# Scan kernel: softplus sums, one-hots, B and a product move to other places and engines

## What is computed

```python
h = layernorm(x);  u, z = split(in_proj(h))           # 256 channels each
uc = silu(causal_conv4(u) + conv_b)
dt, Bm, Cm = split(x_proj(uc))                         # 64, 16, 16
delta = softplus(dt_proj(dt) + dt_bias)
deltaA   = exp(delta * A)                              # 256 channels x 16 states
deltaB_u = delta * Bm * uc
state_t  = deltaA_t * state_{t-1} + deltaB_u_t;  y_t = sum_n state_t * Cm_t
out = out_proj((y + uc * D) * silu(z)) + x
# then: layernorm, 8 experts (128 -> 512 -> 128, gelu), the best two of each token, layernorm
```

## Time and profile before

| | |
|---|---|
| median of 3 runs | 890.92 us (889.49 to 892.53) |
| the profiled execution | 889.88 us, its span 888.0 us |
| VectorE busy | 696.1 us, 78% of the span |
| TensorE busy | 671.0 us, 76% |
| GpSimd busy | 541.4 us, 61% |
| ScalarE busy | 423.7 us, 48% |
| scans (line 1296) | 256, 315.2 us, 1268 ns each |
| inflow (line 1286) | 63, 142.9 us, 2268 ns each |
| times_c (line 533) | 128, 305.9 us, 2395 ns each |
| decay (line 1062) | 256, 164.3 us, 660 ns each |

### The profile page before, as it was taken

The page is one execution under the profiler, slowest core; times in us unless marked ns, Lnnn a source line. Parts: engine busy times, 40 slices in busy tenths (PEclk is TensorE's granted clock), DMA queues, the critical chain, the costliest instruction groups (busy, mean ns, idle before and its releaser), DMA issues. The chain is left out here.

```text
span 888.0 us, 12242 instructions
## 1 busy us (share of the span) xinstructions
PE 671.0 (76%) x2905; PEld 307.3 (35%) x2905; DVE 696.1 (78%) x1350; ACT 423.7 (48%) x884; POOL 541.4 (61%) x526
## 2 busy tenths in 40 slices
PE   3777968797789869878887977887732999999920
PEld 2322212232222223223222222222221888888820
DVE  2167699998998898899889899999732677677754
ACT  3527558366455635736554563334210554445425
POOL 5107547665786776778777677777863455455433
PEclk8876888867886786787787665557555899999975
DMA  3085276374476846627645555565003566566645
GB/s 82 0 203 130 48 163 145 80 178 111 94 176 153 211 119 143 148 51 189 144 103 141 137 137 131 124 147 139 15 32 93 163 179 173 175 172 171 186 130 170
DMA packets 60389, 117.37 MB, mean 132 GB/s; under 512 B 8816, under 2 KB 37296, under 8 KB 52256
## 3 DMA queue, kind: packets, MB, share of 16 engines
q1 hardware_dynamic: 56000, 107.60, 49.4%
q0 software_dynamic: 4320, 8.99, 3.2%
HBM read 100.21 MB, written 16.35 MB: 131 GB/s over the span
## 5 line engine op out<-in xcount | busy, mean ns | idle before, releaser
L533 POOL TENSOR_TENSOR hc<-hs,Crep 128x1024 f32<-128x1024 f32 x128 | 305.9, 2395 | 179.6 <-PE bank L760 83.5
L1296 DVE TENSOR_TENSOR_SCAN hs<-bank,state,flow 128x512 f32<-128x512 f32 x256 | 315.2, 1268 | 41.0 <-ACT bank L1062 35.1
L1062 ACT ACTIVATE bank<-bank,negA 128x512 f32<-128x512 f32 x256 | 164.3, 660 | 247.6 <-PE bank L750 247.4
L750 PE MATMUL bank<-delta,sel 32*128 32x512 f32 x512 | 194.0, 847 | 93.0 <-DVE hs L1296 92.7
L1286 DVE TENSOR_TENSOR flow<-flow,bank 128x2048 f32<-128x2048 f32 x63 | 142.9, 2268 | 6.1 <-PE bank L739 5.7
L750 PEld LDWEIGHTS bank<-delta,sel 32*128 32x128 f32 x512 | 49.8, 238 | 221.9 <-DVE hs L1296 164.8
L1190 ACT ACTIVATE flow<-bank,b1T 128x128 f32<-128x128 f32 x284 | 81.1, 369 | 79.1 <-PE bank L927 79.1
L760 PE MATMUL bank<-hc,kc 128*32 128x512 f32 x512 | 95.4, 830 | 4.5 <-POOL hc L533 4.5
L927 PE MATMUL bank<-flow 128*128 128x128 f32 x568 | 83.0, 291 | 12.8 <-issue 7.6
L642 POOL DMA_INDIRECT results<-flow,idn x71 | 69.8, 983 | 33.2 <-issue 33.2
L699 PE MATMUL bank<-hT,wtapT 128*128 128x512 f32 x128 | 80.5, 751 | 7.1 <-issue 5.1
(11 more groups left out here) (180 smaller groups left out, 790.5 us busy)
## 6 DMA issues: line engine op xcount, KB each, us to landing
flow<-du_d SPq DMA_DIRECT2D x63, 1024.0 KB, 7.2
flow<-L_ffn_W SPq DMA_DIRECT2D x71, 256.0 KB
xg<-xs SPq DMA_DIRECT2D x71, 66.0 KB
hs<-results SPq DMA_DIRECT2D x16, 256.0 KB, 4.3
du_d<-du SPq DMA_DIRECT2D x28, 128.0 KB, 6.6
...
results<-flow,idn POOLq DMA_INDIRECT x71
```

Of the source, the lines that this page charges most:

```text
L533: nc.gpsimd.tensor_tensor(hc[:, Q % 2, two, :], hs[:, Q % 2, two, :], Crep[u % 3][:].unsqueeze(1).broadcast_to([P, 2, T]), ALU.mult).then_ ...
L750: ins = nc.tensor.matmul(dbank[i][:], sel[32 * i:32 * i + 32, q % 4, :], delta[u % 2][32 * i:32 * i + 32, q // 4, :])
L1062: nc.scalar.activation(dbank[G % 4][:], dbank[G % 4][:], ACT.Exp, scale=negA[:, ch:ch + 1]).then_inc(s_ex, 1)
L1296: nc.vector.tensor_tensor_scan(hs[:, Q % 2, j, :], dbank[G % 4][:], flow[Q % 3][:, j, :], state[:, Q // QUADS % 2, Q % QUADS, j:j + 1], AL ...
```

## The change

- VectorE's two softplus sums move from behind scan 13 (21 in unit 0) to behind scan 16 (20).
- The product `delta_u` moves from VectorE (behind scan 14 or 22) to GpSimd (behind times_c of slot 9, or 11 in unit 0).
- The one-hots move from behind scan 30 to behind scan 0 of the next unit; in the last unit they stay.
- `front_stats` moves from g = 25 to 21, `front_rstd` from slot 14 to 12, `relu_plus_exp` from slot 4 to 5 (8 to 7 in unit 0). The eight row lists stand two in a slot in slots 10, 11, 13 and 14.
- `spread_b` moves from g = 0 to g = 29 of the unit before. In program order it stands ahead of proj_x and of the pair of g = 30.
- `fillb` is a tensor of its own. The first times_c doesn't wait for its transfer, and the transfer goes out behind unit 1's spreads.
- On SP, spread_du of the unit's quad 7 stands ahead of store_du.

```diff
--- before.py
+++ after.py
@@ -210,7 +210,7 @@
         is_first = sb("is_first", [P, 8])
         prob = sb("prob", [P, 8])
         tail = sb("tail", [P, E], U32)
-        fillb = hc[:].rearrange("p a j t -> p (a j t)")[:, 0:E * WIDE].rearrange("p (e w) -> p e w", e=E)
+        fillb = sb("fillb", [P, E, WIDE])
         fills = sb("fills", [P, E, WIDE])
 
 
@@ -399,9 +399,6 @@
             spread_du(1)
             store_first_du(1)
             spread_du(2)
-            sp.wait_ge(s_idle, 4)
-            sp.dma_start(xs[bass.ds(E * REGION * P, E * P), :].rearrange("(a p) w -> p a w", p=P), fillb).then_inc(s_fill, 16)
-
             def host(j):
                 nxt = j + 1 < UNITS
                 spread_du(QUADS * j + 3)
@@ -410,14 +407,18 @@
                 if j >= 1 and j + 3 < UNITS:
                     load_x(j + 3)
                 spread_du(QUADS * j + 6)
+                spread_du(QUADS * j + 7)
                 if nxt:
                     store_du(j + 1)
-                spread_du(QUADS * j + 7)
                 if nxt:
                     spread_du(QUADS * j + 8)
                 if nxt:
                     for q in (9, 10):
                         spread_du(QUADS * j + q)
+                if j == 1:
+                    sp.wait_ge(s_idle, 4)
+                    sp.dma_start(xs[bass.ds(E * REGION * P, E * P), :].rearrange("(a p) w -> p a w", p=P), fillb[:])\
+                        .then_inc(s_fill, 16)
                 if j == 2:
                     sp.dma_start(w2_sb[:], W2.rearrange("e (k p) d -> p e k d", p=P)).then_inc(s_w3, 16)
                     sp.dma_start(b2_rep[:], b2.rearrange("e d -> (e d)").partition_broadcast(P)).then_inc(s_w3, 16)
@@ -527,11 +528,13 @@
                 after(pool, s_y, Q - 1)
                 if q == 0 and pair == 0:
                     drained(pool, fill_of(u, "c"))
-                if Q == 0 and pair == 0:
-                    pool.wait_ge(s_fill, 16)
                 two = slice(2 * pair, 2 * pair + 2)
                 nc.gpsimd.tensor_tensor(hc[:, Q % 2, two, :], hs[:, Q % 2, two, :],
                                         Crep[u % 3][:].unsqueeze(1).broadcast_to([P, 2, T]), ALU.mult).then_inc(s_hc, 1)
+
+            def delta_u(u):
+                pool.wait_ge(s_dl, 2 * u + 2)
+                nc.gpsimd.tensor_tensor(du[:], delta[u % 2][:], uc[u % 3], ALU.mult).then_inc(s_du, 2)
 
             def shift_ex(u):
                 pool.wait_ge(s_top, u + 1)
@@ -573,11 +576,13 @@
                 late = j + 1 < UNITS
                 for slot in range(2 * QUADS):
                     times_c(QUADS * j + slot // 2, slot % 2)
-                    if slot == 14 and j + 3 < UNITS:
+                    if slot == 12 and j + 3 < UNITS:
                         front_rstd(j + 3)
                     if j == 0 and slot == 1:
                         front_rstd(2)
-                    if slot == (4 if j else 8) and late:
+                    if slot == (9 if j else 11) and late:
+                        delta_u(j + 1)
+                    if slot == (5 if j else 7) and late:
                         relu_plus_exp(j + 1)
                     if j >= 2:
                         if slot == 1:
@@ -587,12 +592,12 @@
                         if slot == 6:
                             places(j - 2)
                             tag_rows(j - 2)
-                        if slot in (7, 9, 10, 11, 12, 13, 15):
-                            list_rows(j - 2, (7, 9, 10, 11, 12, 13, 15).index(slot))
+                        if slot in (10, 11, 13, 14):
+                            first_row = 2 * (10, 11, 13, 14).index(slot)
+                            list_rows(j - 2, first_row)
+                            list_rows(j - 2, first_row + 1)
                     if slot == 8 and j >= 1:
                         back_rstd(j - 1)
-                    if slot == 15 and j >= 2:
-                        list_rows(j - 2, 7)
 
             front_rstd(0)
             front_rstd(1)
@@ -608,7 +613,7 @@
             for b in range(B):
                 link(nc.gpsimd.memset(xn[b][:], 0.0))
             link(nc.gpsimd.memset(fills[:], 0.0))
-            link(nc.gpsimd.memset(fillb, 0.0))
+            link(nc.gpsimd.memset(fillb[:], 0.0))
             pool.wait_ge(s_w2, 64)
             nc.gpsimd.tensor_copy(fills[:, :, D], spare[:, 0:E]).then_inc(s_idle, 1)
             nc.gpsimd.tensor_copy(fills[:, :, D + 1], lane).then_inc(s_idle, 1)
@@ -806,8 +811,8 @@
                 for g in range(STEPS):
                     if g % 2 == 0:
                         spread_pair((STEPS * j + g) // 2)
-                    if j >= 1 and g == 0:
-                        spread_b(j)
+                    if g == 29 and late:
+                        spread_b(j + 1)
                     if g >= 11 and g % 4 == 3:
                         add_states(QUADS * j + (g - 11) // 4)
                     if g in (3, 7) and j >= 1:
@@ -1246,10 +1251,6 @@
                 nc.vector.scalar_tensor_tensor(delta[u % 2][:], delta[u % 2][:], 0.0, relu[:], ALU.min, ALU.add)\
                     .then_inc(s_dl, 2)
 
-            def delta_u(u):
-                dve.wait_ge(s_dl, 2 * u + 2)
-                nc.vector.tensor_tensor(du[:], delta[u % 2][:], uc[u % 3], ALU.mult).then_inc(s_du, 2)
-
             def first_delta():
                 for h in range(HALVES):
                     d = delta[0][:, h, :]
@@ -1365,13 +1366,15 @@
 
             def host(j):
                 late = j + 1 < UNITS
-                add_at, du_at = (13, 14) if j else (21, 22)
+                add_at = 16 if j else 20
                 for g in range(STEPS):
                     if g % 4 == 0:
                         inflow(QUADS * j + g // 4)
                     scan(STEPS * j + g)
                     if j == 0 and g == 2:
                         front_stats(2)
+                    if g == 0 and j >= 2:
+                        one_hots(j - 2)
                     if g == 6 and j >= 2:
                         ranks(j - 2)
                     if g == 7 and j >= 1:
@@ -1380,19 +1383,17 @@
                         place(j - 2)
                     if g == add_at and late:
                         add_log(j + 1)
-                    if g == du_at and late:
-                        delta_u(j + 1)
                     if g == 16 and j >= 1:
                         residual(j - 1)
                     if g == 17 and j >= 1:
                         back_stats(j - 1)
                     if g == 23:
                         post(j, 0)
-                    if g == 25 and j + 3 < UNITS:
+                    if g == 21 and j + 3 < UNITS:
                         front_stats(j + 3)
                     if g == 29 and j >= 1:
                         best_two(j - 1)
-                    if g == 30 and j >= 1:
+                    if g == 30 and j == UNITS - 1:
                         one_hots(j - 1)
 
             dve.wait_ge(s_w2, 64)
```

## The result

The changed kernel took 893.96 us at the median (891.27 to 902.75), the one before 890.9 in the same comparison: a ratio of 1.0047, 95% interval 1.0031 to 1.0063. It is slower by half a per cent, where 882 with a range of 866 to 892 had been forecast. The profiled execution took 897.15 us, its span 895.3, against 889.88 and 888.0; it is 3.2 us above the median of its kernel, so what only one unit of it shows need not be in every execution.

The account below looks back on a forecast made before the run. The prediction took VectorE to set the pace, with TensorE second. Its terms, from -11.9 us for the softplus sums to +8.0 for B in units 1 to 5, summed to -9.0 us: 882 on the median, range 866 to 892.

Parts of the forecast that it names:

- one_hots at -2.1: One-hots behind the next unit's first scan: unit 6's collision goes, -2.1 us; in units 2 to 5 ScalarE waits cover it, 0.
- B at +9.6: Replicating B at g = 29 stops TensorE and delays scans 30 and 0: +8.0, +1.1 and +0.5 us.
- VectorE sets the pace: Mid-scan units: VectorE busy 68.1 of 75.0 us, so work taken off it is worth its length unless another chain sets the next scan.
- The lock of the two engines: Softplus sums: VectorE and GpSimd exclude each other; behind the quad's first scan six collisions of 1.98 us go.
- the +1.0 for unit 0: Product in unit 0's slot 11: du spread by 131 or 132, VectorE ready at about 130, charged +1.0 us.
- The chain at the edge: Unit's end: TensorE stops 1 to 2 us, then B, proj_x and pairs at half clock; scan 0 +1.6 us in units 1 to 5.
- The sums (-11.9 + 5.2): Softplus sums: six second-sum collisions go, -11.9 us; the first sum waits 1.05 us for times_c five times, +5.2.
- The product (-9.1): Moving line 1251's product to GpSimd frees VectorE about 1.1 us six times and about 2.5 once: -9.1 us.
- The buffer (-1.2): Own buffer for spare rows: GpSimd's first times_c starts sooner, so ScalarE's 1.25 us wait at 75.02 goes, -1.2 us.
- Rival (b): TensorE's half clock carries past the unit's edge: +2.4 us in five units, 894 us; chance 0.12.
- Rival (c): Collisions only move: each sum meets a whole times_c (+6.5 us), one-hots held beyond cover (+4), 892.5 us; chance 0.13.
- Rival (a): B costs nothing: TensorE at full clock at the unit's end, -1.5 instead of +1.6 us five times, 866.5 us; chance 0.25.

Follow-up runs that it names:

- the two corners with one_hots moved: The changed kernel with spread_b put back at g = 0, ratio 0.994, and the changed kernel itself, 1.0047, each against the kernel before.

## Why the prediction was wrong

**The steps that failed.** Two terms: one_hots at -2.1, taken as covered, which measures +15 us, and B at +9.6, which by itself measures +24. Behind both stands the step "VectorE sets the pace": with neither of the two moved, a unit is 71.5 us and VectorE idle for 6.5 of them, about as before (6.9), but with them units 2 and 3 kept their 75 us.

**What held.** The lock of the two engines and its end at scan 16: 1226 ns in six of seven. The product at 2.35 us and no inflow waiting for du outside unit 1's first, which waits 0.19 at 130.03; VectorE's ready time of 130 was right, and the +1.0 for unit 0 was 0.2. The chain at the edge: TensorE stops for the inflow at g = 29 (not ahead of unit 5, where it was late anyway), scan 30 waits, 13.7 us to scan 0 forecast and 14.1 to 15.1 measured.

**The sums (-11.9 + 5.2).** The +5.2 was wrong. GpSimd's and VectorE's rows of the changed kernel:

```profile
313.25 2.36 POOL L532 TENSOR_TENSOR hc<-hs,Crep 128x1024 f32<-128x1024 f32 x1
```

```profile
315.51 1.20 DVE L1247 SCALAR_TENSOR_TENSOR delta<-du,delta 128x1024 f32<-128x1024 f32 x1
316.80 1.23 DVE L1251 SCALAR_TENSOR_TENSOR delta<-delta,relu 128x1024 f32<-128x1024 f32 x1
```

Slot 7 of GpSimd started 1.2 us behind scan 15 (which ended at 312.0) and not 2.2, since places and tag_rows were through in 1.1 us once nothing held them: the 1.18 us in the earlier trace rows for the first of them had been a collision too. The line is held by 0.2 and 0.3 us, not by 1.05 five times. With the product behind scan 17 the part was worth -12.7 alone.

**one_hots (-2.1).** This is the largest miss of the change without B, and it is one of an assumption: the cover was read in the trace of before, where it exists (0.9989 alone), and the same change removes it. By the ratios it costs some 15 us with B at g = 0, where the bound in the text was 8. The profiled execution of that kernel has the comparison held by 1.8 to 2.6 us in five units, and its span is longer by 7.6 us; where the rest of the 15 goes, no trace shows. The -2.1 of unit 6 wasn't gained in the changed kernel either: the comparison moved to the start of unit 7 and is held there (2.62 us at 579.49).

**B (+9.6).** Between the two corners with one_hots moved it measures +9.5. That agreement is an accident: there B displaces a cost that one_hots had already put at the edge. By itself it is +21.6 us in the kernel before and +24 in the changed one. The edge term, +1.6 a unit, was nearly right against 12.1 (+2.1). Its terms were less so: the 1.0 us for B was an estimate from half a pair, and B by itself takes 2.04 to 2.07, while the stop is 1.0 to 1.15, the lower end of the 1 to 2. The text didn't see either that B at g = 0 ran beside the pair, at no time of its own. Behind the edge, more was missing: in the kernel before, the chain through rstd, xhat and the decay of scan 2; in the changed one, 0.9 and 0.7 us in quads 0 and 1, 1.4 in quad 6 with its longer low stretch, and the low clock carried over at one edge of five.

**The small terms.** The product (-9.1) measures -7.1 with a wide interval, and none of it in units 2 to 5. The buffer (-1.2) is 0. front_stats was rightly 0 by itself, and the price of moving it was the cover of one_hots.

**The sum.** Terms were added that aren't independent. Without B and one_hots the text has -9.1 - 11.9 + 5.2 - 1.2 - 0.45 + 1.0 = -16.5, and the kernel measured -20.4. Then one_hots put +15 on it, and B +24 less the 15 that it hides. "VectorE sets the pace" failed as a step: VectorE lost 3.1 us of work a unit, and units 2 and 3 kept their 75 us because of B's place and TensorE's low clock; with B and one_hots put back they last 71.2 and 71.5.

**The rivals.** Rival (b) gave 894, with the low clock carried over, and the measured time is 894. It happened at one edge of five (427.3 to 439.6) at a cost of 4.8 us, not five times at 2.4; so that its number came out is luck. Rival (c) named the collision of one_hots, which then showed mostly with B put back. Rival (a) was refuted.

**Open.** Why the low stretch ahead of quad 6 is 10.2 us in one unit and 6.8 in the next, and why at the same edge of the same program the low clock is carried over in one unit and not in another, isn't settled. How much of one_hots' 15 us is the missing cover and how much the row lists ahead of the last times_c wasn't tried.
